# Low-rank experts in pairs of tiles: earlier gate logits, a second routing behind the first tile's sums, ups in front of downs

## The reference

```python
logits = einsum('bsd,ed->bse', x, Wg) + bg            # E = 4 experts
topv, topi = top_k(softmax(logits), 2)
w = sum(one_hot(topi, E) * topv[..., None], axis=-2)  # weight of each expert, two of them zero
base = einsum('bsd,fd->bsf', x, Wi)                   # F = 512
lora = einsum('bser,efr->bsef', einsum('bsd,erd->bser', x, A), B)
h = relu(base[:, :, None, :] + lora)
out = einsum('bse,bsed->bsd', w, einsum('bsef,df->bsed', h, Wo))
```

## Time and profile before

| | |
|---|---|
| median of 3 runs | 1577.67 us (1577.65, 1577.67, 1581.76) |
| profiled execution | 1580.86 us, its span 1579.1 us |
| mean granted clock of TensorE | 0.96 |
| busy: PE, DVE, ACT, POOL | 1359.9, 1096.8, 748.0, 340.2 us |
| chain that ended last | PE 56%, DVE 24%, ACT 7%, issue 6%, POOL 2% |
| L1277 (ups) in that chain | 3% |

### The profile page before, as it was taken

The page is one execution under the profiler, slowest core; times in us unless marked ns, Lnnn a source line. Parts: engine busy times, 40 slices in busy tenths (PEclk is TensorE's granted clock), DMA queues, the critical chain, the costliest instruction groups (busy, mean ns, idle before and its releaser), DMA issues.

```text
span 1579.1 us, 28502 instructions
## 1 busy us (share of the span) xinstructions
PE 1359.9 (86%) x10940; PEld 898.5 (57%) x10940; DVE 1096.8 (69%) x3269; ACT 748.0 (47%) x1418; POOL 340.2 (22%) x282
## 2 busy tenths in 40 slices
PE   4788987897997998798798898889789899888967
PEld 4455744565664764466475575446556567445745
DVE  3566975877667786686765687677766669758774
ACT  0154544774244633575334554467433455357632
POOL 1021310540130230261003021044012113015300
PEclk7799999999999989999899999999999999999999
DMA  9000000000000000000000000000000000000000
GB/s 356 5 2 1 1 1 1 1 1 17 1 8 1 1 1 1 1 1 2 17 1 8 1 1 1 1 1 2 17 2 7 1 1 1 1 1 2 1 1 8
DMA packets 15095, 18.96 MB, mean 12 GB/s; under 512 B 2776, under 2 KB 13672, under 8 KB 14444
## 3 DMA queue, kind: packets, MB, share of 16 engines
q1 hardware_dynamic: 14960, 17.13, 3.2%
HBM read 16.08 MB, written 1.05 MB: 11 GB/s over the span
## 4 chain that ended last, share of the span: by engine, by line
PE 56%; DVE 24%; ACT 7%; issue 6%; POOL 2%; DVEq 0%; POOLq 0%; ACTq 0%
PE bank L1048 7%; PE bank L1059 5%; PE bank L1436 4%; PE bank L1441 4%; PE bank L1277 3%; DVE work L644 3%; DVE small L643 3%; PE bank L1829 2%; PE bank L856 2%; DVE small L650 2%; PE bank L351 2%; PE bank L1429 2%; PE bank L1472 2%; PE bank L502 2%; PE bank L1847 2%
## 5 line engine op out<-in xcount | busy, mean ns | idle before, releaser
L267 POOL TENSOR_TENSOR root<-variance,minus_half 128x2 f32<-128x2 f32 (+1 forms) x72 | 55.2, 767 | 693.8 <-DVE variance L284 426.8
L1101 ACT ACTIVATE work<-bank,w_f 128x512 f32<-128x512 f32 x128 | 87.9, 687 | 93.9 <-PE bank L1048 93.6
L1059 PEld LDWEIGHTS bank<-w_f1d,work 128*128 128x128 f32 x1024 | 119.1, 192 | 13.5 <-issue 13.5
L1048 PE MATMUL bank<-xnT,w_f 128*128 128x512 f32 x256 | 121.8, 623 | 0.0
L1059 PE MATMUL bank<-w_f1d,work 128*128 128x129 f32 x1024 | 119.9, 275 | 0.0
L1610 ACT ACTIVATE work<-work,small 128x128 f32<-128x128 f32 x256 | 78.3, 388 | 84.8 <-DVE small L1737 84.8
L1668 POOL TENSOR_TENSOR small<-small 128x16 f32<-128x16 f32 x32 | 92.9, 2902 | 106.5 <-DVE small L1696 104.9
L1695 DVE TENSOR_REDUCE small<-work 128x16 f32<-128x1024 f32 x48 | 58.4, 1217 | 40.4 <-ACT work L1574 38.7
L643 DVE TENSOR_REDUCE small<-bank 128x8 f32<-128x512 f32 x96 | 65.5, 682 | 30.0 <-PE bank L510 30.0
L1436 PE MATMUL bank<-w_x,cxT 128*128 128x512 f32 x128 | 62.3, 608 | 21.8 <-DVE work L1709 17.0
L1441 PEld LDWEIGHTS bank<-consts,work 128*128 128x128 f32 x576 | 64.2, 140 | 29.2 <-issue 16.8
(11 more groups left out here) (281 smaller groups left out, 3162.4 us busy)
## 6 DMA issues: line engine op xcount, KB each, us to landing
w_f<-in_f_dram SPq DMA_DIRECT2D x1, 2616.0 KB
w_f<-in_f_dram SPq DMA_DIRECT2D x1, 2180.0 KB, 25.4
w_x<-in_x_dram SPq DMA_DIRECT2D x1, 2115.0 KB
w_l<-in_l_dram SPq DMA_DIRECT2D x1, 2088.5 KB, 20.5
w_f1d<-in_f1d_dram SPq DMA_DIRECT2D x4, 512.0 KB
work<-in_x_dram SPq DMA_DIRECT2D x4, 256.0 KB, 2.8
work<-in_ctx_dram SPq DMA_DIRECT2D x4, 256.0 KB, 3.5
out_dram<-x SPq DMA_DIRECT2D x4, 256.0 KB, 2.3
```

The costliest lines, as they stand in the source:

```text
L1048: pe.matmul(banks[n % 3][:, :], k_f1["w1"][:, e * 512 + c * P:e * 512 + (c + 1) * P], xnT[:, :], start=True, stop=True).then_inc(up_done, 1)
L1059: pe.matmul(z_of(e, t)[:, 0:129], hT[e % 2][:, c, t * P:(t + 1) * P], w_f1d[:, c, e, :], start=(c == 0), stop=(c == 3))
L1101: act.activation(hT[e % 2][:, c, :], banks[n % 3][:, :], ACT.Relu, bias=k_f1["b1"][:, n:n + 1]).then_inc(hT_ready, 1)
```

## The change

- `FILL_BEFORE_ROWS[4]` goes from 3 to 0.
- The rows are turned, copied and routed by pairs. TensorE turns pair 0 (L371, into bank 4), makes its gate logits (L1270, bank 6), runs the ups of two experts of tile 0, turns pair 1 (bank 5), runs a third, makes the logits of pair 1 (bank 7), and goes on with the fourth expert and tile 1. The routing (`routing(pair)`) is done for two tiles at a time, with `comb_ready` signalled twice.
- ScalarE applies the relus of tile 0 without a weight. VectorE weights them in its sum: a product with the weight (L1389) and three multiply-adds (L1393) for tile 0. The second routing stands behind that sum on VectorE, and the exponents of pair 1 between two relus of tile 1 on ScalarE.
- The ups of tile t+2 stand between turn t and downs t.
- VectorE's norm of pair 0 stands behind tile 3's sum and no longer around its first add, and its last step behind the update of x of tile 2.

In the code, cut to the engines' orders:

```diff
-FILL_BEFORE_ROWS = (0, 0, 0, 2, 3, 0, 0, 3)
+FILL_BEFORE_ROWS = (0, 0, 0, 2, 0, 0, 0, 3)
...
-                    turn_pairs(pe, prev, turn_no, xn)
-                    wait_for(pe, prev.all_used)
-                    pe.wait_ge(rowsT_ready, due(rowsT_ready, 2 * turn_no + 2))
...
+                    def down(t):
                         pe.wait_ge(gT_ready, due(gT_ready, t + 1))
+                        pe.wait_ge(comb_ready, due(comb_ready, t % 2 + 1))
...
-                    for t in range(TILES + 1):
-                        if t < TILES:
-                            up(t)
-                        if t == 0:
-                            pe.wait_ge(comb_ready, due(comb_ready, 1))
-                        if t >= 1:
-                            turn(t - 1)
+                    turn_pair(pe, turn_no, xn, 0, banks[4])
+                    wait_for(pe, prev.all_used)
+                    route(0)
+                    up(0, (0, 1))
+                    turn_pair(pe, turn_no, xn, 1, banks[5])
+                    up(0, (2,))
+                    route(1)
+                    up(0, (3,))
+                    up(1, range(4))
+                    for t in range(TILES):
+                        turn(t)
+                        if t + 2 < TILES:
+                            up(t + 2, range(4))
+                        down(t)
...
-                    take_pairs(act, turn_no)
-                    act.wait_ge(shifted, due(shifted, 1))
-                    act.activation(ex, shifted_lg, ACT.Exp).then_inc(exp_ready, 1)
+                            weight = 1.0 if t == 0 else comb[:, t, e:e + 1]
+                            act.activation(r[t % 2][e], banks[e][:, :], ACT.Relu, scale=weight).then_inc(r_ready, 1)
...
+                    take_pair(act, turn_no, 0, banks[4])
+                    relus(0, (0, 1))
+                    take_pair(act, turn_no, 1, banks[5])
+                    exps(0)
+                    relus(0, (2, 3))
                     act.wait_ge(comb_ready, due(comb_ready, 1))
...
+                    relus(1, (0, 1))
+                    exps(1)
+                    relus(1, (2, 3))
+                    for t in range(TILES):
+                        take(t)
+                        if t + 2 < TILES:
+                            act.wait_ge(comb_ready, due(comb_ready, 2))
+                            relus(t + 2, range(4))
...
+                    def add_experts(t):
+
+                        acc = r[t % 2][0]
+                        dve.wait_ge(r_ready, due(r_ready, 4 * t + 2))
+                        if t == 0:
+                            link(dve.tensor_scalar(acc, acc, comb[:, t, 0:1], None, ALU.mult))
+                        for e in (1, 2, 3):
+                            dve.wait_ge(r_ready, due(r_ready, 4 * t + e + 1))
+                            if t == 0:
+                                ins = dve.scalar_tensor_tensor(acc, r[t % 2][e], comb[:, t, e:e + 1], acc, ALU.mult, ALU.add)
+                            else:
+                                ins = dve.tensor_tensor(acc, acc, r[t % 2][e], ALU.add)
...
+                    routing(0)
                     next_rows = iter(())
                     for t in range(TILES + 1):
+                        if t < TILES:
+                            add_experts(t)
+                        if t == 0:
+                            routing(1)
                         some(next_rows, 3)
-                        if t < TILES:
-                            dve.wait_ge(r_ready, due(r_ready, 4 * t + 2))
-                            link(dve.tensor_tensor(r[t % 2][0], r[t % 2][0], r[t % 2][1], ALU.add))
-                            some(next_rows, 1)
```

More of the change, by code:

```diff
@@ L1254, in ffn2 @@
             tmp = small[:, 272:288].rearrange("p (t e) -> p t e", t=TILES)
+            best = small[:, 160:192].rearrange("p (t s) -> p t s", t=TILES)
+            where = small[:, 192:224].bitcast(U32).rearrange("p (t s) -> p t s", t=TILES)
+            place = small[:, 224:232].rearrange("p (t s) -> p t s", t=TILES)
             r = [[work[:, 2048 * i + 512 * e:2048 * i + 512 * e + 512] for e in range(4)] for i in range(2)]
@@ L1263, in _, with route, up @@
                 def _(pe):
-                    turn_pairs(pe, prev, turn_no, xn)
-                    wait_for(pe, prev.all_used)
-                    pe.wait_ge(rowsT_ready, due(rowsT_ready, 2 * turn_no + 2))
[L1267 to L1273, removed]
+                    def route(pair):
+                        pe.wait_ge(rowsT_ready, due(rowsT_ready, 2 * turn_no + pair + 1))
+                        for t in pair_tiles(pair):
+                            m = pe.matmul(banks[6 + pair][:, t * 4:(t + 1) * 4], xnT[:, t * P:(t + 1) * P], k_f2["wg"],
+                                          start=True, stop=True)
+                        m.then_inc(routed, 1)
+                    def up(t, experts):
+                        for e in experts:
                             n = 4 * t + e
@@ L1307, in _, with relus @@
-                    act.wait_ge(shifted, due(shifted, 1))
-                    act.activation(ex, shifted_lg, ACT.Exp).then_inc(exp_ready, 1)
-                    act.wait_ge(comb_ready, due(comb_ready, 1))
-                    for t in range(TILES + 1):
-                        if t < TILES:
[L1312 to L1323, removed]
+                    def relus(t, experts):
+                        for e in experts:
+                            act.wait_ge(up_done, due(up_done, 4 * t + e + 1))
+                            if t >= 2 and e == 0:
+                                act.wait_ge(turned, due(turned, t - 1))
+                            weight = 1.0 if t == 0 else comb[:, t, e:e + 1]
+                            act.activation(r[t % 2][e], banks[e][:, :], ACT.Relu, scale=weight).then_inc(r_ready, 1)
@@ new lines, in exps, with take @@
+                    def exps(pair):
+                        own = slice(2 * pair, 2 * pair + 2)
+                        act.wait_ge(shifted, due(shifted, pair + 1))
+                        act.activation(ex[:, own, :], shifted_lg[:, own, :], ACT.Exp).then_inc(exp_ready, 1)
+                    def take(t):
+                        act.wait_ge(turned, due(turned, t + 1))
+                        if t >= 2:
+                            act.wait_ge(down_done, due(down_done, t - 1))
+                        act.copy(gT[t % 2], banks[4 + t % 2][:, :]).then_inc(gT_ready, 1)
@@ L1333, in _ @@
                     link(dve.memset(lg, NEG))
[L1334 to L1338, removed]
-                                          ALU.subtract).then_inc(shifted, 1)
@@ L1341, in _ @@
[L1341 to L1347, removed]
@@ new lines, in add_experts @@
+                    def add_experts(t):
[9 more added lines that the diff above has]
+                                ins = dve.tensor_tensor(acc, acc, r[t % 2][e], ALU.add)
+                            if e == 3:
+                                ins.then_inc(sum_ready, 1)
+                            else:
+                                link(ins)
@@ L1369, in body @@
                 ends.append(Ends((r_ready, 14), (taken, 4)))
-            stage("routed:1 shifted:1 expd:1 comb:1 up:16 r:16 sum:4 turned:4 gT:4 down:4 taken:4", body)
+            stage("routed:2 shifted:2 expd:2 comb:2 up:16 r:16 sum:4 turned:4 gT:4 down:4 taken:4", body)
             return ends[0]
```

26 lines of the change are left out of this document (20 added, 6 removed).

## The result

The changed kernel takes 1565.44 us (1564.73 to 1567.37, four runs), the one before 1579.72 (1577.65 to 1590.46, four runs, three of them those shown ahead): a ratio of 0.9898, interval 0.9851 to 0.9945. I had forecast 1559.4, 1556 to 1563 as its own range, and 1554 to 1568 for eight in ten. The time lies above the first range and inside the second. The profiled spans are 1563.5 and 1579.1. So it is faster, by some 14 us where I had 18, and the time is that of my first rival (1565.1).

The account below looks back on a forecast made before the run. Bound: the chain of waits, mostly TensorE, then VectorE. 1580.86 less 19.2 (four blocks of 3.5 + 1.3) plus 0.9 gave 1562.6; with the median 3.2 lower, 1559.4, range 1556 to 1563, eight in ten 1554 to 1568.

Parts of the forecast that it names:

- my first rival: Head of the low-rank experts: the clock falls in every block, 4 x 1.65 on top of 1558.5, giving 1565.1; 16%.
- part 1: Stage head: pair 0 turned and ups begun while VectorE still norms pair 1, gaining 3.5 us a block.
- The one delay I had found: Stage head on ScalarE: pair 1's copy comes behind expert 1's relu, at 245.87 against 245.54 before.
- parts 2 and 3: Rest of the stage: ups between turn and downs, pair 0's norm behind the sums; together 1.3 us a block.
- rival (b): VectorE's fused multiply-adds take 1.22 each, so first sum and second routing become the chain: 3.8 more, 1563.2; 8%.
- part 4: Stage head without idle products: one clock fall expected, +1.65, less 0.76 regained in block 2: +0.9 us.
- One of my own signs of being wrong: Stage head: ups at 0.85 a record would show the forecast wrong.
- (a): Clock falls in the head of every block, 4 x 1.65 on top of 1558.5: 1565.1; 16%.
- my 19.2: Low-rank expert stage, all four blocks: gain of the new order before any clock effect, 4.8 us a block.
- (c): Head starts no earlier because a wait holds the gate products until pair 1 is there; 1.3 left, 1572.5; 4%.
- (d): Slower: one long clock fall in each block's ups, 12 us at 0.50 costing 6.0 a block, 1582.5; 4%.

Follow-up runs that it names:

- downs behind turns: Changed kernel with each tile's downs put directly behind its transposes again, ups of tile t+2 behind them; 1576.80 us, ratio to before 0.9984.
- the second profile: The changed kernel run once more with nothing altered, to see its spread; 1566.63 us, ratio to before 0.9892.
- tail with 768 columns: Changed kernel plus 768 columns of idle products in each of TensorE's last two waits in the attention ahead; 1555.75 us, ratio to before 0.9848.
- the norm between the adds: Changed kernel with pair 0's norm back around the first add of tile 3; 1589.30 us, ratio to before 1.0059.

## Why the prediction was right, and where it was not

**The head (part 1), 3.5.** Right. In block 2 the ups start 1.43 behind the start of pair 0's turn (617.49 to 618.92), as in my sum (241.91 to 243.34), and no sum or routing was late. The one delay I had found, pair 1's copy behind a relu, is there. With downs behind turns the head, with the norm's new place, gives 26.64 less some 23.0 to 23.2 (estimated above): 3.4 to 3.6.

**The order and the norm (parts 2 and 3), 1.3.** Right in sum: with the head they gave 26.64 - 21.48 = 5.16 against my 4.8. VectorE's wait of 2.36 for tile 1's downs and TensorE's for the last sum (0.35, where I had 0.6) stand where I had worked them out. The multiply-adds took 0.752 each (9.0 us for 12), beside the 0.744 I took and far from the 1.22 of rival (b).

**The idle products (part 4), +0.9.** This is the term that was wrong. I wrote: "But here TensorE gets real 512-column products at 243.34, where there it had none, so I expect one fall". There were three in one profile and four in the other, two of the three and all of the four about 6.8 us long, twice the 3.3 that I took. What a fall costs I had right, about half its length; how many there would be and how long they would last I had not. The two falls that I priced from lasted 3.4 us each in the kernel before, and the one of block 2 shows the half: its six records of idle products, 2.43 us of them before the clock is back at 621.8, took 3.95 where block 1's took 2.74, 1.21 more. The kernel before, timeline and windows:

```profile
619.38 3.95 PE L351 MATMUL bank<-w_x,consts 128*128 128x512 f32 x6
```

```profile
126.90:130.30 3.40, 3.40 (x18) 1.90 (x18) 2.27 (x11) 0.60 (x1) 0.69 (x1) 0.50 0.00 0
618.40:621.80 3.40, 3.00 (x5) 1.60 (x6) 2.33 (x11) 0.00 (x0) 0.69 (x1) 0.50 0.00 0
```

The three falls in the changed kernel cost 3.15 + 2.99 + 1.68 = 7.8 where I had 1.65, and the 0.76 of the old block 2 came back: +7.1 in place of +0.9. One of my own signs of being wrong, slow ups in the head, stood in three blocks of four.

The dense ups stand too late in block 1 to have kept the fall away: it is there at 242.2, before the first of them (242.97), behind the sparse tail of the attention (busy 1.59 of 3.5 us). Without the clock the stage gave 4 x 5.16 = 20.6, with it 13.5; in the second profile the falls cost 97.74 - 4 x 21.48 = 11.8.

What my first rival went by, the border without idle products and a sparse TensorE at the attention's end, was nearer to what came. The runs show where a fall starts at this border and what keeps it away: the clock fell in 22 of the 24 heads without idle products (six profiles of five kernels), in one of four with them in the head (in each of two kernels), in two of four with the shorter ones in the tail, and in none of the twelve with the longer ones (three kernels). How a fall ends the runs leave open: it went on for 6.40 us of work without a gap.

**Rivals.** (a) came true, at 1565.1 against 1565.44; it had the price of short falls in four blocks (6.6), and the traces have 7.8 in three blocks and 11.8 in four. That the time agrees within 0.4 us is luck: the order gave 1.4 more than my 19.2, some 2 us came from outside the stage, and the profiled execution before was slower than its median where the one after was not. The wide range held because I had put this rival into it. (c) and (d) didn't occur: the gate products started at once, and no fall in a head of the changed kernel lasted more than some 7 us (heads with falls of 10 us and more stood only in the old order without idle products: 10.2 in three blocks, 13.7 in one). A fall also makes the first routing wait for its exponents (1.74), which I had not seen; it stayed covered by tile 1's ups.

**Open.** Why some falls last twice as long as others in the same head, and why block 2's head had none behind a tail as sparse as block 1's, was not tried. The 2 us between 13.5 in the stage and 15.6 in the spans were not traced; falls in other places may be their cause. These differ between two profiles of the changed kernel: from 522.1 to 525.5 the clock was 1.00 in the first and 0.50 in the second.

## What to carry to other kernels

When an edit makes a stretch of TensorE's list sparse, or takes idle products out, look at the granted clock of the border in every pass of the profile, and price the falls by their number and their length: here each cost up to half its length (3.15 of 6.8 us, 1.68 of 3.4), and the forecast failed on how many and how long. A wait of another engine behind such a fall costs nothing while it stays covered (here VectorE's 1.74 for the exponents); look for the next instruction that needs its result. An idle product belongs in a wait of TensorE for another engine, short enough to end before it: there it cost nothing, in front of ready work it cost 2.3 of its 2.7 us. After a reordering, read each engine's list for an instruction that waits in front of ready work; here the update of x of tile 1 held three adds, and setting them ahead, with turn 3, was worth 1.55 a block.

## What the runs showed of the hardware

- Taking three idle products (2.7 us) out of each of four places cost the program 13 us by the medians (1590.3 against 1577.4).
- A fall can go on while TensorE has an instruction at work all the time: 6.40 of 6.40 us busy at 0.50 (changed kernel, block 1).
- In the heads of the changed kernel falls of some 6.8 us cost 2.3 to 3.2 us of the pass (3.15, 2.99, and 2.27 where it began earlier), one of some 3.4 us 1.68.
- Without falls the same stage repeated within 0.02 us over four blocks (21.48 to 21.50, tail with 768 columns); with them the changed kernel's passes went from 21.48 to 24.69, so nearly all of that spread is the clock.
- With the norm between the adds, TensorE's wait of 2.50 us stood ahead of a second fall, at the next border, in each of the four blocks (a clock of 0.57 from 650 to 658 in block 2). In the changed kernel that wait was 0.35 in block 2 and no fall stood there.
